# Attention block: the softmax denominators' partial sums shared anew between VectorE and GpSimd, and the unit's order laid out again

## The chip, the core and the metric

One NeuronCore of a Trainium2 chip runs the whole kernel. It has a matrix engine (TensorE), a vector engine (VectorE), an activation engine (ScalarE), a general engine (GpSimd) and SyncE, from whose queue all DMAs are issued here. Each engine works through its own instructions in order and waits on semaphores. The metric is the device time of one execution in microseconds (us).

## The reference

```python
x = L0_attn_q                                   # (4, 1024, 128)
xn = layernorm(x)
xq, xk, xv = rope(xn @ Wq), rope(xn @ Wk), xn @ Wv   # 16 heads of 64; k and v have half the width
xk, xv = repeat(xk, 2, axis=-1), repeat(xv, 2, axis=-1)
scores = softmax(xq @ xk * scale, axis=-1)      # per head, 1024 queries by 1024 keys
attn = (scores @ xv) @ Wo
ffn = (silu(xn @ w_gate.T) * (xn @ w_up.T)) @ w_down.T
return x + attn + ffn
```

Everything is float32. The repetition doubles equal columns, so the kernel works with 32 dimensions per head.

## The kernel before

**Stages.** Up to about 110 us the kernel normalises, transposes x, makes the feed-forward part and the first projections. Then come 32 units (`UNITS`, numbered u): four batches, four groups of four heads, two halves of 512 queries. The loops are unrolled, and each engine has a function `slot` that lists its work for one unit. Unit 31 (`LAST`) has lists of its own.

**One unit.** There are eight tiles of 128 keys (kt = 0 to 7) and four heads (h). TensorE computes the scores of tile kt and head h into one of two PSUM banks (`score`, L553); a score waits until the exponential two before it has read the bank. ScalarE writes exp(score) to `prob` (L871), a ring of four key tiles. TensorE multiplies a finished tile with v (`pv`, four heads side by side, L407). The row maxima of the *next* unit are made beside this: 16 maxima a unit, each from two matmuls (`max_tile`, L392) into one of two places, read by VectorE's row maximum (`reduce_tile`, L950); maximum matmul m waits until maximum m-2 is read. VectorE then splits the maxima into a high and a low part (`split_max`: a cast at L956, a difference at L958), TensorE transposes them (L399), and a DMA puts them beside the queries. The unit also makes projections for a unit three or four later (`project_chunk`, L374; `project_v`, L382), which VectorE rotates (`rotate`, six operations, L941 to L945), ScalarE rounds to a high part (`round_hi`, L757, two halves) and GpSimd subtracts to a low part (`split_lo`, L1125, two halves). SyncE packs both into the score operands.

**The denominators.** A row's denominator is the sum of its exponentials over eight key tiles. Before the change GpSimd adds tiles 0 and 1 (L1173), then 2, then 3; VectorE adds tiles 4 and 5 to `prob_pair` (`pair_sum`, L1043), GpSimd adds this pair and then tile 6 (all L1181). Tile 7 is not added: TensorE sums over the keys with a matrix of ones in two passes, tile 7 (L417) and the partial sum (L420). Behind it come a copy (`read_den`), a transposition (L427), the inversion on VectorE (`invert`, behind row maximum `INVERT_AFTER`), a spread, a transposition back (L434), the product with the output (`normalise`, behind row maximum `NORMALISE_AFTER`) and, one unit later, the output projection (`project_out`, L443), which ScalarE copies (`read_y`) and GpSimd adds (`add_out`, L1189).

**What sets the order.** It is written out by hand in `slot`, engine by engine, with semaphore waits. A ring tile of `prob` may be overwritten when P·V and the partial sums have read it: before, exponentials of tiles 0 and 1 wait for the pair, of tile 2 for the whole sum of the unit before, of tile 3 for its denominators. `prob_pair` is a single buffer. On GpSimd a unit's list is: both low halves, the output add, five large adds.

## Time and profile before

| | |
|---|---|
| median of 3 runs | 1128.86 us (1128.25 to 1129.79) |
| the profiled execution | 1127.29 us |
| its span, first to last instruction | 1125.4 us |
| granted TensorE clock over the span | 0.991 of full speed |
| busy: TensorE, VectorE, GpSimd, ScalarE | 1090.5, 912.1, 853.3, 722.1 us |
| a middle unit | 31.63 us |

A profile shows one execution. Its busy time is a mean over stages, so the table of stretches and the timelines below are read for one unit. Recorded times of instructions overlap a little at their ends: of two neighbours the distance between their starts tells the cost.

### The profile page before, as it was taken

To read this page: it belongs to the slowest core of one execution; us is meant where nothing else is said; L and a number is where in the kernel's file an instruction comes from. 1 tells how busy PE (TensorE), PEld (TensorE's weight loads), DVE (VectorE), ACT (ScalarE), POOL (GpSimd) and SP (SyncE) were. 2 spreads that over 40 slices of the span, in tenths; PEclk is the share of its full clock that TensorE was granted. 3 is DMA by queue.
4 is the path that set the end of the run, shared out by engine and by line. 5 is a ranking of instruction groups with operands and counts; after the bars stand their busy time and mean duration, and the time that the engine had idled before them with its cause. 6 is when DMAs were issued, how large, how long until landed. Compare 5 with 4: busy or idle time off the path is not lost.

```text
span 1125.4 us, 17086 instructions
## 1 busy us (share of the span) xinstructions
PE 1090.5 (97%) x6288; PEld 661.9 (59%) x6288; DVE 912.1 (81%) x1023; ACT 722.1 (64%) x1327; POOL 853.3 (76%) x268
## 2 busy tenths in 40 slices
PE   5899999999999999999999999999999999999987
PEld 4787455666656565656656565656666565654533
DVE  7686878888888888888888888888888888887755
ACT  3333666666666676667666676667666676666664
POOL 3321878888888888888888888888888888888770
PEclk9899999999999999999999999999999999999998
DMA  6662907144260817154260817153260817140000
GB/s 238 159 246 101 269 1 196 38 150 121 48 186 2 232 38 205 29 142 129 50 183 2 232 38 205 29 155 117 51 183 2 232 38 202 32 109 26 4 2 19
DMA packets 56338, 124.98 MB, mean 111 GB/s; under 512 B 8000, under 2 KB 19520, under 8 KB 54080
## 3 DMA queue, kind: packets, MB, share of 16 engines
q1 hardware_dynamic: 56256, 123.90, 37.8%
q8 instruction: 51, 0.84, 0.3%
q14 instruction: 31, 0.25, 0.1%
HBM read 53.08 MB, written 10.49 MB: 56 GB/s over the span
## 4 chain that ended last, share of the span: by engine, by line
PE 93%; DVE 4%; ACT 2%; DMA 1%; issue 1%; ACTq 0%; DVEq 0%
PE bank_s L553 24%; PE scores L392 22%; PE bank_o L407 21%; PE scores L374 8%; PE bank_m L382 3%; PE bank_m L417 3%; PE bank_m L420 2%; PE bank_m L443 2%; PE scores L493 2%; PE bank_s L510 1%; PE bank_m L427 1%; PE bank_m L434 1%; DVE row_max L950 1%; PE bank_o L510 1%; PE bank_m L510 1%
## 5 line engine op out<-in xcount | busy, mean ns | idle before, releaser
L871 ACT ACTIVATE prob<-bank_s 128x512 f32<-128x512 f32 x992 | 566.2, 599 | 274.0 <-PE bank_s L553 263.9
L950 DVE TENSOR_REDUCE row_max<-scores 128x1 f32<-128x1024 f32 x512 | 601.2, 1215 | 97.0 <-PE scores L392 92.9
L1181 POOL TENSOR_TENSOR prob_sum<-prob_sum,prob 128x2048 f32<-128x2048 f32 x93 | 427.1, 4592 | 13.4
L553 PE MATMUL bank_s<-qk_pack 98*128 98x512 f32 x992 | 393.4, 427 | 3.4 <-ACT prob L871 2.0
L392 PE MATMUL scores<-qk_pack 96*128 96x512 f32 x1024 | 323.4, 402 | 2.4 <-DVE rope L945 1.7
L553 PEld LDWEIGHTS bank_s<-qk_pack 98*128 98x128 f32 x992 | 178.2, 188 | 176.2 <-ACT prob L871 117.5
L407 PE MATMUL bank_o<-prob,v 128*32 128x512 f32 x2048 | 254.4, 603 | 0.0
L392 PEld LDWEIGHTS scores<-qk_pack 96*128 96x128 f32 x1024 | 184.6, 189 | 61.1 <-DVE row_max L950 28.8
L1181 POOL TENSOR_TENSOR prob_sum<-prob_sum,prob_pair 128x2048 f32<-128x2048 f32 x31 | 142.5, 4596 | 80.9 <-DVE prob_pair L1043 80.9
L1173 POOL TENSOR_TENSOR prob_sum<-prob 128x2048 f32<-128x2048 f32 x31 | 142.2, 4587 | 0.0
L1125 POOL TENSOR_TENSOR qk_stage<-rope,qk_stage 128x512 fp32r<-128x512 f32 x64 | 81.8, 1280 | 77.9 <-ACT qk_stage L757 77.8
L407 PEld LDWEIGHTS bank_o<-prob,v 128*32 128x32 f32 x2048 | 50.5, 109 | 112.4 <-issue 89.4
L374 PE MATMUL scores<-x_stage,w_stage 128*128 128x512 f32 x336 | 96.7, 396 | 0.0
L374 PEld LDWEIGHTS scores<-x_stage,w_stage 128*128 128x128 f32 x336 | 63.7, 190 | 14.7
L1043 DVE TENSOR_TENSOR prob_pair<-prob 128x2048 f32<-128x2048 f32 x31 | 70.8, 2284 | 0.0
L1189 POOL TENSOR_TENSOR y_acc<-y_part,y_acc 128x512 f32<-128x512 f32 x31 | 39.6, 1278 | 23.2 <-ACT y_part L849 23.2
L1047 DVE RECIPROCAL den_inv<-bank_m 128x16 f32<-128x16 f32 x31 | 8.0, 258 | 60.5 <-PE bank_m L427 60.5
L382 PEld LDWEIGHTS bank_m<-w_stage,x_stage 128*128 128x128 f32 x336 | 46.2, 191 | 4.8
L941 DVE TENSOR_TENSOR scores<-scores,table 128x512 f32<-128x512 f32 x64 | 44.2, 691 | 2.5 <-PE scores L374 2.5
L945 DVE TENSOR_TENSOR rope<-scores,rope 128x512 f32<-128x512 f32 x64 | 44.2, 691 | 2.2
L382 PE MATMUL bank_m<-w_stage,x_stage 128*128 128x128 f32 x336 | 43.8, 267 | 0.0
L943 DVE TENSOR_TENSOR rope<-scores,table 128x512 f32<-128x512 f32 x64 | 43.6, 681 | 0.1
(105 smaller groups left out, 754.3 us busy)
## 6 DMA issues: line engine op xcount, KB each, us to landing
qk_pack<-qk_stage SPq DMA_DIRECT2D x384, 128.0 KB, 4.5
table<-tables SPq DMA_DIRECT2D x16, 2048.0 KB, 9.7
w_stage<-w_scratch SPq DMA_DIRECT2D x14, 640.0 KB, 4.7
v<-v_stage SPq DMA_DIRECT2D x32, 256.0 KB, 7.4
xT_scratch<-xT_hl SPq DMA_DIRECT2D x4, 1024.0 KB, 9.2
x_stage<-xT_scratch SPq DMA_DIRECT2D x4, 1024.0 KB, 6.6
w_scratch<-w_split SPq DMA_DIRECT2D x1, 2560.0 KB, 15.1
x_all<-x SPq DMA_DIRECT2D x4, 512.0 KB, 11.7
```

The costliest lines, as they stand in the source:

```text
L374: last = mm(scores[:, c, :], w_from[:, a, c, :], x_from[:, r, cols], start=n == 0, stop=n == 2)
L382: last = mm(bank_m[:, j * 128:(j + 1) * 128], x_from[:, r, at:at + 128], w_from[:, a, 4, :], start=n == 0, stop=n == 2)
L392: last = mm(scores[:, 2 * (m % places) + c, :], qk_pack[n][0:SPLIT_K, 0, t, h, (m % QT) * 128:(m % QT + 1) * 128], qk_pack[n][0:SPLIT_K, 1 ...
L407: last = mm(bank_o[h * E:(h + 1) * E, :], v_sb[n][:, kt, h * E:(h + 1) * E], prob[:, kt % RING, h, :], start=kt == 0, stop=kt == KT - 1)
L553: mm(bank_s[:, h % 2, :], qk_pack[j][0:SCORE_K, 1, kt // QT, h, (kt % QT) * 128:(kt % QT + 1) * 128], qk_pack[j][0:SCORE_K, 0, t, h, :], s ...
L871: A(prob[:, kt % RING, h, :], bank_s[:, h % 2, :], ACT.Exp).then_inc(prob_ready, 1)
L941: V.tensor_tensor(scores[:, 2 * k, :], scores[:, 2 * k, :], table[:, t, 2 * k, :], ALU.mult).then_inc(rope_read, 1)
L950: V.tensor_reduce(row_max[:, m:m + 1], scores[:, at:at + 2, :].rearrange("p c k -> p (c k)"), axis=AX.X, op=ALU.max).then_inc(max_read, 1)
L1043: V.tensor_tensor(prob_pair[:], prob[:, 4 % RING], prob[:, 5 % RING], ALU.add).then_inc(pair_done, 1)
L1125: TT(qk_stage[:, 2 * k + 1, t, :], rope[:, 2 * k, :], qk_stage[:, 2 * k, t, :].bitcast(F32), ALU.subtract).then_inc(lo_done, 1)
L1173: TT(prob_sum[:, t], prob[:, 0], prob[:, 1], ALU.add).then_inc(sum_done, 1)
L1181: TT(prob_sum[:, t], prob_sum[:, t], part, ALU.add).then_inc(sum_done, 1)
```

## The change

VectorE gets a second pair a unit, tiles 6 and 7 (`last_pair_sum`), into the same buffer `prob_pair`; it stands behind the first row maximum of the next unit and waits until GpSimd has added the first pair. GpSimd no longer adds tile 6 alone; it adds the second pair in the next unit, between the two low halves. The output add moves behind the first large add. The denominators are one pass over the finished sum. The waits of the exponentials follow: tiles 0 and 1 wait for the first pair of the unit before, tiles 2 and 3 for its second pair. `pv` of tile 6 moves with tile 7 into the next unit; TensorE's maxima, P·V groups, transpositions and projections are put in another order; ScalarE's roundings and copies come at other exponentials; the inversion comes behind row maximum 10 and the normalisation behind 15.

```diff
-INVERT_AFTER = 7
-NORMALISE_AFTER = 14
+INVERT_AFTER = 10
+NORMALISE_AFTER = 15
...
 def denominators(u, t):
-                for h in range(HG):
-                    mm(bank_m[h * E:(h + 1) * E, :], ones[:], prob[:, (KT - 1) % RING, h, :], start=True, stop=False)
                 pe.wait_ge(sum_done, 5 * u + 5)
                 for h in range(HG):
-                    last = mm(bank_m[h * E:(h + 1) * E, :], ones[:], prob_sum[:, t, h, :], start=False, stop=True)
+                    last = mm(bank_m[h * E:(h + 1) * E, :], ones[:], prob_sum[:, t, h, :], start=True, stop=True)
...
-                def pv_last():
+                def pv_rest():
                     if not is_first(u):
+                        pv(u - 1, KT - 2, j if t == 1 else 1 - j)
                         pv(u - 1, KT - 1, j if t == 1 else 1 - j)
...
 ScalarE, exponentials:
                         if kt < 2:
-                            act.wait_ge(pair_done, u)
-                        elif kt == 2:
-                            act.wait_ge(sum_done, 5 * u)
-                        elif kt == 3:
-                            act.wait_ge(den_ready, u)
+                            act.wait_ge(pair_done, 2 * u - 1)
+                        elif kt < 4:
+                            act.wait_ge(pair_done, 2 * u)
...
-                        if (kt, h) == (0, 2) and staged:
+                        if (kt, h) == (0, 0) and staged:
                             round_hi(0, u + 3, 1 - t, s + 1 + t)
...
+                        elif (kt, h) == (0, 3) and staged:
+                            round_hi(1, u + 3, 1 - t, s + 1 + t)
...
 VectorE:
+            def last_pair_sum(u):
+
+                dve.wait_ge(prob_ready, NE * KT * (u + 1))
+                dve.wait_ge(sum_done, 5 * u + 4)
+                V.tensor_tensor(prob_pair[:], prob[:, 6 % RING], prob[:, 7 % RING], ALU.add).then_inc(pair_done, 1)
...
                 for m in range(TILES):
                     reduce_tile(u + 1, m)
+                    if m == 0 and not is_first(u):
+                        last_pair_sum(u - 1)
...
 GpSimd:
+            def add_pair(u, t, n):
+
+                pool.wait_ge(pair_done, 2 * u + 1 + n)
+                pool.wait_ge(sum_done, 5 * u + 3 + n)
+                TT(prob_sum[:, t], prob_sum[:, t], prob_pair[:], ALU.add).then_inc(sum_done, 1)
...
-                if not (last_pair and (j, t) != (0, 0)):
-                    split_lo(u + 3, 1 - t)
+                staged = not (last_pair and (j, t) != (0, 0))
+                if staged:
+                    split_lo(u + 3, 1 - t, range(0, 1))
+                if not is_first(u):
+                    add_pair(u - 1, 1 - t, 1)
+                if staged:
+                    split_lo(u + 3, 1 - t, range(1, 2))
+                add_first(u, t)
                 if not is_second(u):
                     add_out(u - 2, t, (u - 2) // UNITS_B)
-                add_probs(u, t)
+                add_next(u, t)
+                add_pair(u, t, 0)
```

TensorE's new order of a unit, where S is a score (tile, head), M a maximum, PV a P·V, D the denominators, V half of the v projection, O the output projection, C a projection chunk, T a transposition, and M0' the first maximum of the unit after next:

```
0: S00 S01 M1 V S02 M2 S03 PV6 PV7 (of the unit before)
1: S10 M3 S11 M4 S12 O S13 M5
2: S20 M6 S21 D M7 S22 S23 M8 PV0
3: S30 M9 S31 T(den) S32 M10 S33 M11
4: S40 PV1 S41 M12 S42 M13 S43 T(inv)
5: S50 M14 S51 S52 M15 S53 PV2 PV3
6: S60 S61 C0 C1 T(max) S62 S63 C2 C3
7: S70 S71 PV4 PV5 S72 S73 M0' V
```

## Rows read from the trace of the kernel before

**Rows 1.** The page's first part: busy time and share of each engine.

```profile
PE 1090.5 (97%) x6288; PEld 661.9 (59%) x6288; DVE 912.1 (81%) x1023; ACT 722.1 (64%) x1327; POOL 853.3 (76%) x268
```

**Rows 2.** Units 1, 10, 28, 29: length, busy time by engine, clock, DMA share, GB/s.

```profile
141.87:173.41 31.54, 31.50 (x180) 17.91 (x179) 25.89 (x28) 21.19 (x39) 24.22 (x7) 1.00 0.01 2
426.47:458.10 31.63, 31.63 (x187) 18.96 (x187) 26.73 (x28) 21.68 (x40) 26.68 (x9) 1.00 0.73 206
995.81:1026.25 30.44, 29.30 (x169) 15.81 (x169) 23.08 (x23) 21.11 (x40) 25.49 (x9) 1.00 0.51 124
1026.25:1056.23 29.98, 29.46 (x161) 15.11 (x162) 22.03 (x22) 20.00 (x38) 24.75 (x7) 1.00 0.01 4
```

**Rows 3.** Timeline of TensorE in unit 10: start, duration, line, tiles, count.

```profile
435.01 1.06 PE L417 MATMUL bank_m<-prob,ones 128*32 128x512 f32 x8
435.89 1.04 PE L420 MATMUL bank_m<-prob_sum,ones 128*32 128x512 f32 x8
...
446.42 0.48 PE L553 MATMUL bank_s<-qk_pack 98*128 98x512 f32 x1
...
447.21 0.40 PE L553 MATMUL bank_s<-qk_pack 98*128 98x512 f32 x1
```

**Rows 4.** Timeline of VectorE where units 9 and 10 meet, and in the tail.

```profile
419.17 1.13 DVE L956 CAST max_hl<-row_max 128x16 fp32r<-128x16 f32 x1
...
420.43 2.28 DVE L1043 TENSOR_TENSOR prob_pair<-prob 128x2048 f32<-128x2048 f32 x1
...
426.48 2.35 DVE L950 TENSOR_REDUCE row_max<-scores 128x1 f32<-128x1024 f32 x2
...
1095.64 2.97 DVE L1081 TENSOR_TENSOR prob_sum<-prob_sum,prob 128x2048 f32<-128x2048 f32 x1 [0.78 <-ACT prob L915]
```

**Rows 5.** Timeline of GpSimd over units 9 and 10.

```profile
403.73 1.28 POOL L1125 TENSOR_TENSOR qk_stage<-rope,qk_stage 128x512 fp32r<-128x512 f32 x1 [2.00 <-ACT qk_stage L757]
...
406.21 4.59 POOL L1173 TENSOR_TENSOR prob_sum<-prob 128x2048 f32<-128x2048 f32 x1
410.94 9.34 POOL L1181 TENSOR_TENSOR prob_sum<-prob_sum,prob 128x2048 f32<-128x2048 f32 x2
422.80 4.60 POOL L1181 TENSOR_TENSOR prob_sum<-prob_sum,prob_pair 128x2048 f32<-128x2048 f32 x1 [2.52 <-DVE prob_pair L1043]
427.54 4.59 POOL L1181 TENSOR_TENSOR prob_sum<-prob_sum,prob 128x2048 f32<-128x2048 f32 x1
432.09 1.28 POOL L1125 TENSOR_TENSOR qk_stage<-rope,qk_stage 128x512 fp32r<-128x512 f32 x1
```

**Rows 6.** By line: shortest, median, longest (ns), first and last start; two timeline rows.

```profile
L956 DVE CAST max_hl<-row_max x32: 174/1134/1161, 101.3 to 1080.4; 128x16 fp32r<-128x16 f32 x32
...
1095.18 1.28 POOL L1189 TENSOR_TENSOR y_acc<-y_part,y_acc 128x512 f32<-128x512 f32 x1 [2.85 <-ACT y_part L849]
...
L1130 POOL TENSOR_TENSOR w_split<-w_raw,w_split x3: 1569/1577/1706, 15.3 to 18.9; 128x640 fp32r<-128x640 f32 x3
...
14.63 0.96 DVE L1013 TENSOR_TENSOR wgu<-y_acc,wgu 128x768 fp32r<-128x768 f32 x1 [0.63 <-ACT wgu L787]
...
L950 DVE TENSOR_REDUCE row_max<-scores x512: 1161/1215/1226, 45.5 to 1079.1; 128x1 f32<-128x1024 f32 x171
```

**Rows 7.** Timeline: two scores on TensorE, their exponentials, a high part's cast on ScalarE.

```profile
411.06 0.70 PE L553 MATMUL bank_s<-qk_pack 98*128 98x512 f32 x2
...
411.57 1.09 ACT L871 ACTIVATE prob<-bank_s 128x512 f32<-128x512 f32 x2 [0.37 <-PE bank_s L553]
...
429.06 0.61 ACT L757 CAST qk_stage<-rope 128x512 fp32r<-128x512 f32 x1
```

**Rows 8.** Timeline of the last unit: denominators, score, exponential.

```profile
1095.16 1.43 PE L417 MATMUL bank_m<-prob,ones 128*32 128x512 f32 x8 [2.02 <-ACT y_part L849]
...
1098.22 1.15 PE L685 MATMUL bank_s<-qk_pack 98*128 98x512 f32 x2
1099.13 1.08 ACT L915 ACTIVATE prob<-bank_s 128x512 f32<-128x512 f32 x2 [3.52 <-PE bank_s L685]
```

More of the change, by code:

```diff
@@ L592, in slot @@
                     if kt == 0:
+                        score(kt, 1)
                         if is_first(u):
@@ L596, in slot @@
                         maximum(1)
-                        score(kt, 1)
                         second_half_v()
@@ L601, in slot @@
                         score(kt, 3)
+                        pv_rest()
+                    elif kt == 1:
                         maximum(3)
-                    elif kt == 1:
-                        pv_last()
+                        score(kt, 1)
                         maximum(4)
-                        score(kt, 1)
-                        maximum(5)
                         score(kt, 2)
@@ L611, in slot @@
                         score(kt, 3)
+                        maximum(5)
+                    elif kt == 2:
                         maximum(6)
-                    elif kt == 2:
-                        maximum(7)
                         score(kt, 1)
@@ L617, in slot @@
                             denominators(u - 1, 1 - t)
+                        maximum(7)
                         score(kt, 2)
@@ L620, in slot @@
                         maximum(8)
+                        pv(u, 0, j)
+                    elif kt == 3:
+                        maximum(9)
+                        score(kt, 1)
                         if not is_first(u):
                             transpose_den(u - 1)
-                        maximum(9)
-                    elif kt == 3:
-                        score(kt, 1)
-                        pv(u, 0, j)
-                        pv(u, 1, j)
+                        score(kt, 2)
+                        maximum(10)
+                        score(kt, 3)
+                        maximum(11)
+                    elif kt == 4:
+                        pv(u, 1, j)
+                        score(kt, 1)
+                        maximum(12)
+                        score(kt, 2)
+                        maximum(13)
+                        score(kt, 3)
+                        if not is_first(u):
+                            transpose_inv(u - 1)
+                    elif kt == 5:
+                        maximum(14)
+                        score(kt, 1)
+                        score(kt, 2)
+                        maximum(15)
+                        score(kt, 3)
+                        pv(u, 2, j)
+                        pv(u, 3, j)
+                    elif kt == 6:
+                        score(kt, 1)
+                        project_chunk(0)
+                        project_chunk(1)
+                        at_least(pe, o_done, u)
+                        transpose_max(v)
@@ L653, in slot @@
                         project_chunk(2)
-                        score(kt, 3)
                         project_chunk(3)
-                        at_least(pe, o_done, u)
-                        transpose_max(v)
                     else:
                         score(kt, 1)
-                        for n in (4, 5, 6):
-                            pv(u, n, j)
+                        pv(u, 4, j)
+                        pv(u, 5, j)
                         score(kt, 2)
@@ L1083, in last_slot @@
             def last_slot():
+                last_pair_sum(LAST - 1)
                 dve.wait_ge(den_ready, LAST - 1)
@@ L1120, in _, with split_lo @@
             TT = nc.gpsimd.tensor_tensor
-            def split_lo(w, t):
-                for k in range(2):
+            def split_lo(w, t, halves=range(2)):
+                for k in halves:
                     pool.wait_ge(hi_done, 2 * w + k + 1)
@@ L1173, in add_probs, with add_next @@
                 TT(prob_sum[:, t], prob[:, 0], prob[:, 1], ALU.add).then_inc(sum_done, 1)
-                for n, kt in enumerate((2, 3, 4, 6)):
-                    if kt == 4:
-                        pool.wait_ge(pair_done, u + 1)
-                    else:
-                        pool.wait_ge(prob_ready, NE * (KT * u + kt + 1))
-                    pool.wait_ge(sum_done, 5 * u + n + 1)
-                    part = prob_pair[:] if kt == 4 else prob[:, kt % RING]
-                    TT(prob_sum[:, t], prob_sum[:, t], part, ALU.add).then_inc(sum_done, 1)
+            def add_next(u, t):
+                for n, kt in enumerate((2, 3)):
+                    pool.wait_ge(prob_ready, NE * (KT * u + kt + 1))
+                    pool.wait_ge(sum_done, 5 * u + n + 1)
+                    TT(prob_sum[:, t], prob_sum[:, t], prob[:, kt % RING], ALU.add).then_inc(sum_done, 1)
+            def add_pair(u, t, n):
+                pool.wait_ge(pair_done, 2 * u + 1 + n)
+                pool.wait_ge(sum_done, 5 * u + 3 + n)
+                TT(prob_sum[:, t], prob_sum[:, t], prob_pair[:], ALU.add).then_inc(sum_done, 1)
             def add_out(u, t, b):
@@ L1205, in _ @@
             pairs_of_steps(body)
+            add_pair(LAST - 1, 0, 1)
             add_out(LAST - 2, 1, B - 1)
```

54 lines of the change are left out of this document (13 added, 41 removed).

## The prediction

> **What bounds the kernel now.** I read the page's busy shares first: TensorE is busy 97% of the span, VectorE 81%, GpSimd 76%, ScalarE 64% [rows 1]. The table of stretches then shows where that holds. In a middle unit (one head group, half the queries) TensorE is busy for all of its 31.63 us, at the full granted clock, while VectorE has 26.73 and GpSimd 26.68 us of work [rows 2]. So today the unit is as long as TensorE's list, and each of the other two has 4.9 us to spare. The reader should not stop there: spare time helps only where no order of waits uses it up. So I went on to the timelines of VectorE and GpSimd and looked for a ring of work that runs through both.
>
> **What TensorE saves.** The first four-head pass of the denominators (eight instructions) begins 0.88 us before the second [rows 3]; the change leaves one pass. Nothing else leaves TensorE: the second P·V of the last pair of tiles only moves into the next unit, and there are five P·V groups in a unit before and after, so the switches between P·V and score matmuls stay the same in number. TensorE's list becomes 31.63 - 0.88 = 30.75 us. The new order adds waits of its own. A score's bank is free again only when its exponential is done: that starts 0.51 us after the score and takes 0.60 (of a pair 1.09 us long, the second ends 0.5 after the first) [rows 7]. Scores 0 and 2 of stage 5 now have one score and one maximum between them, and a score and a maximum take 0.79 us together [rows 3], so with the second score about 1.0; the bank needs about 1.2. I take 0.3 us a unit for this and the score behind it (estimate; ends 0, if the loads run ahead, and 0.9). **TensorE alone: about 31.05 us.** If that were the bound, 26 middle units (2 to 27) would give back 26 x 0.58 = 15 us.
>
> **What VectorE gets.** One more add of 128x2048, which lasts 2.28 us as the present pair does [rows 4]: 26.73 + 2.28 = 29.01 us, still under 31.05. It stands behind the first row maximum of the next unit, with fifteen maxima queued behind it, on which TensorE's maximum matmuls 3 and 4 wait. The inversion, for which VectorE today stands idle, moves from behind maximum 7 to behind maximum 10, so this idle time pays for most of the pair.
>
> **What GpSimd gets.** The same five large adds and three small ones; a pair takes the place of tile 6. But the pair's add moves into the next unit, between the two halves of the low-part subtraction (I call them lo0 and lo1). GpSimd waits there for VectorE, with lo1, the first add and all of the unit's sum queued behind it; the one denominator pass on TensorE waits for it in turn. No DMA is moved; SyncE packs a head when lo1 is done, which comes at about the same place of the unit as before, and lo0 earlier.
>
> **Two engines at one door.** The cast of the row maxima (16 columns) takes 0.174 us at its shortest and 1.134 in the median [rows 6]. In the middle unit it begins at 419.17, lasts 1.13 and ends at 420.30 [rows 4]; GpSimd's adds of tiles 2 and 3 end at 410.94 + 9.34 = 420.28 [rows 5]. In the tail a VectorE add with both inputs in SBUF lasts 2.97 us where the pair lasts 2.28 [rows 4]; it begins at 1095.64, inside a GpSimd add that runs from 1095.18 to 1096.46 [rows 6]. So VectorE's cast and its SBUF+SBUF adds stand still until about 0.15 us before the GpSimd operation ends. The other way round there is one row: GpSimd's first weight subtraction starts at 15.3, while a VectorE add with two SBUF inputs runs until 15.59, and takes 1.706 us where the others take 1.57 [rows 6]: it ends at VectorE's end plus its own length less 0.14. The row maxima, which read PSUM, show no such stretch: 1161 to 1226 ns from the shortest to the longest [rows 6].
>
> The Trainium skill says the same of the mechanism (SBUF — State Buffer, § Who interferes with whom): a VectorE instruction with two SBUF inputs contends with a GpSimd instruction that reads SBUF, and the one that comes second fully blocks. It speaks against this change, which puts a second such add into the one stretch where GpSimd has something ready to run. Both directions agree with rows 6; without the rule the sum would be TensorE's 31.05.
>
> **Who meets whom now.** In the new order the second pair starts on VectorE about 1 us into the unit. lo0 needs the first exponential (0.51 + 0.6) and the high part's cast behind it (0.61) [rows 7], so it is ready at about 1.7 and finds VectorE in the middle of its 2.28 us. lo0 therefore ends at the pair's end + 1.28 - 0.14 = +1.14, and the pair's add on GpSimd starts 1.10 us behind VectorE's end, not 0.09 (today's step from 420.43 + 2.28 = 422.71 to 422.80 [rows 4, 5]).
>
> **The ring, step by step**, from the start of the pair's add on GpSimd: this add 4.55 (427.54 to 432.09 [rows 5]); lo1 1.24 (two small operations take 403.73 to 406.21, 2.48); the first add 4.55; the output add 1.24; tiles 2 and 3, 9.34. Sum 20.92. Behind its end: cast, difference, first pair and rope run without a gap on VectorE until the next row maximum, 420.28 to 426.48 = 6.20 [rows 4, 5]. Then that maximum 1.15 (two take 2.35), the second pair 2.28, and 1.10 to the next start. **20.92 + 6.20 + 1.15 + 2.28 + 1.10 = 31.65 us.** A second ring, through GpSimd's own add of the first pair (7.12 from 420.28 to 427.40) in place of rope and maximum, gives 20.92 + 7.12 + 0.09 + 2.28 + 1.10 = 31.51. So the bound passes from TensorE (31.63) to a ring through GpSimd and VectorE of the same length, and TensorE gets waits of about 0.5 us a unit, at the transposition of the maxima above all, which waits for the late cast. **A middle unit stays at 31.63, within 0.1.** What the denominators give back is lost again before the cast.
>
> **The ends.** Unit 1 has no output add, so its ring is 31.65 - 1.24 = 30.4 where it took 31.54 [rows 2]: -1.1. Unit 28 has no projection to fill TensorE but still lo0 and lo1: from the second pair's end, the transposition comes at 4.5 + 20.92 + 0.4 = 25.8 behind the first maximum, and the last scores, P·V and exponentials behind it take about 5.4 (estimate from the same spacings): 31.1 against 30.44 [rows 2]: +0.7. Units 29 and 30 have no lo0 and lo1, so the ring is shorter there by more than 2 us and TensorE bounds them: 0.88 saved, about 0.5 of it lost behind the second pair, against 29.98 today [rows 2]: -0.4 each, -0.8. In the last unit TensorE waits 2.02 us in front of the denominators, and the pass from 1095.16 to 1098.22 takes 3.06 us; the exponentials of tile 3 follow at 1099.13 [rows 8]. Half a pass goes (some 1.4 us), one more P·V pushes the scores ahead of it back by about as much as the wait leaves over: -1.0 (ends -2.5 and +0.5). Unit 0 is unchanged. **Together -2.2 us.**
>
> The profiled execution took 1127.29 us, a span of 1125.40 and 1.89 around it; the median of the runs is 1128.86, 1.57 above. 1127.29 - 2.2 = 1125.1 in such an execution, **1126.6 as a median; I say 1126.5.**
>
> **Rivals.** (a) *GpSimd is not held while VectorE adds the pair.* Only 0.28 us of overlap in one row speaks for the hold in that direction. Then the step of 1.10 is 0.09, the ring 30.64, and TensorE bounds at 31.05: 26 x -0.58 = -15, with the ends some -16 to -17: 1112. (b) *The hand-over is dearer.* If lo0 runs its whole length behind the pair, a unit has 0.14 more: +3.6 - 2.2, 1130.3. It decides from 0.17 us a unit: (2.2 + 2.3) / 26.
> The Trainium skill's figure, in the same page (§ A bandwidth-pool intuition that's wrong), is a start about 115 ns behind VectorE's end; that would be 0.26 a unit and 1133; no row here shows it.
> (c) *TensorE loses its slack* and ends slower: the second pair holds maxima 1 and 2 back by 2.2 us, maximum matmuls 3 and 4 wait for them, and VectorE, with 29 us of work, cannot catch up, so later maxima, the exponentials' banks and the denominators come late together. Price: all waits of TensorE beyond 0.9 a unit; it is slower from 0.17 above that. At 1.2, the unit is 31.95: 26 x 0.32 - 2.2 = +6.1, 1135. For it: two lists of 29 and 31 us in lock step with two score buffers. Against: by the order written out, each maximum finds its buffer read. (d) *It does not do what it says*: the denominators' one pass waits for a sum that comes later than today's. It is due at about 9 us of the unit and the ring has the sum at 4.5 + 4.6 = 9.1: under 0.2, inside TensorE's slack; no case of its own.
>
> **Chances.** Forecast ring 0.58 (0.28 faster, 0.27 inside 0.2%, 0.03 slower); (a) 0.15, faster; (b) 0.13 (0.05 same, 0.08 slower); (c) 0.10 (0.02 same, 0.08 slower); the rest 0.04 (0.02 faster, 0.02 slower). Faster 0.45, same 0.34, slower 0.21; 0.2% (2.3 us) is about what a measurement of this kernel can tell from no change. The likeliest case alone holds 1124 to 1130; the range reaches to (a) and to the near part of (b) and (c): 1112 to 1132.
>
> **What would show it.** Middle units of 31.5 to 31.8; GpSimd's lo0 drawn out or begun behind VectorE's second pair; the cast still ending with GpSimd's add of tile 3; TensorE waiting for the difference of the maxima. If middle units are at 31.1 with lo0 inside the pair, (a) is right; if the maxima wait for TensorE and TensorE for the maxima, (c).

## The result, and the profile after

The changed kernel takes 1135.59 us (median of 20 executions, 1128.61 to 1144.03) where the kernel before takes 1129.23 (20, 1127.81 to 1135.23): the ratio is 1.0055, with a 95% interval of 1.0037 to 1.0073. It is slower by half a per cent; the forecast was 1126.5, with a range up to 1132. The execution that was profiled took 1132.50 us with a span of 1130.7, 5.3 more than the span before.

The page's first part, as in [rows 1]:

```profile
PE 1084.1 (96%) x6040; PEld 649.0 (57%) x6040; DVE 1007.9 (89%) x1054; ACT 718.8 (64%) x1327; POOL 887.7 (79%) x268
```

TensorE has lost 248 instructions (a pass of 8 in each of 31 units), VectorE has 31 more. The stretches that answer to [rows 2], cut at the same instruction (the first score behind the next unit's first maximum matmul and its value projection, where there is one; I call that maximum M0', a unit's own M1 to M15): units 1, 10, 28, 29 and 30. Columns: length, busy time of TensorE, its loads, VectorE, ScalarE and GpSimd, then the granted clock, DMA share and GB/s.

```profile
142.80:176.91 34.11, 34.00 (x171) 19.25 (x171) 27.89 (x29) 21.38 (x39) 26.29 (x7) 0.90 0.00 1
429.76:461.42 31.66, 31.25 (x179) 18.42 (x179) 29.91 (x29) 21.51 (x40) 27.96 (x9) 1.00 0.74 206
999.11:1031.71 32.60, 30.19 (x162) 15.54 (x161) 26.00 (x23) 21.22 (x40) 28.52 (x9) 0.95 0.47 116
1031.71:1061.63 29.92, 28.99 (x153) 14.74 (x154) 24.46 (x23) 20.36 (x38) 23.25 (x6) 1.00 0.01 4
1061.63:1093.17 31.54, 30.19 (x152) 14.55 (x152) 24.46 (x22) 20.37 (x38) 24.89 (x7) 0.95 0.01 2
```

Unit 30 of the kernel before, by the same cut, had a stretch at the lower clock too:

```profile
1056.23:1087.84 31.61, 30.61 (x159) 15.00 (x160) 21.99 (x21) 20.02 (x38) 25.65 (x8) 0.95 0.00 1
```

With the starts of the units this gives the whole balance. The last column is an experiment's, told below.

| us against the kernel before | forecast | changed | changed, M0' waiting for head 0 only |
|---|---|---|---|
| up to unit 1 (141.87 before) | 0 | +0.93 | -1.99 |
| unit 1 (31.54) | -1.1 | +2.57 | -0.54 |
| units 2 to 27 together (822.40) | 0 | -0.20 | -0.23 |
| unit 28 (30.44) | +0.7 | +2.16 | +1.89 |
| unit 29 (29.98) | -0.4 | -0.06 | 0.00 |
| unit 30 (31.61) | -0.4 | -0.07 | -1.69 |
| last unit (37.56) | -1.0 | -0.03 | +0.06 |
| span (1125.4) | -2.2 | +5.3 | -2.5 |

Each kernel was profiled once more later. Units 1 and 28 of those executions by the same cut, first of the changed kernel, then of the kernel before:

```profile
142.16:176.32 34.16, 34.05 (x172) 18.78 (x171) 27.81 (x29) 21.41 (x39) 26.52 (x7) 0.90 0.00 1
998.40:1029.36 30.96, 28.54 (x161) 15.38 (x161) 26.03 (x23) 21.22 (x40) 27.25 (x9) 1.00 0.50 122
```

```profile
142.12:173.68 31.56, 31.52 (x180) 17.88 (x179) 25.87 (x28) 21.17 (x39) 24.53 (x7) 1.00 0.01 2
997.37:1029.48 32.11, 30.99 (x170) 16.13 (x169) 23.06 (x23) 21.10 (x40) 27.17 (x9) 0.95 0.48 118
```

Unit 1 is longer in the changed kernel in both pairs (+2.57 and +2.60). Unit 28 is not: it was +2.16 and is -1.15, and it is long in whichever execution has the lower clock there. Up to unit 1 the pairs differ by +0.93 and +0.04.

**The middle is as forecast.** VectorE, GpSimd and TensorE of the changed kernel, where units 10 and 11 meet and a little later:

```profile
462.35 2.28 DVE L1044 TENSOR_TENSOR prob_pair<-prob 128x2048 f32<-128x2048 f32 x1
463.17 2.60 POOL L1129 TENSOR_TENSOR qk_stage<-rope,qk_stage 128x512 fp32r<-128x512 f32 x1 [1.04 <-ACT qk_stage L757]
...
465.73 4.59 POOL L1190 TENSOR_TENSOR prob_sum<-prob_sum,prob_pair 128x2048 f32<-128x2048 f32 x1
...
477.30 9.33 POOL L1184 TENSOR_TENSOR prob_sum<-prob_sum,prob 128x2048 f32<-128x2048 f32 x2
...
484.40 2.27 DVE L951 CAST max_hl<-row_max 128x16 fp32r<-128x16 f32 x1
...
487.02 0.27 PE L399 MATMUL bank_m<-ident,max_hl 128*32 128x128 f32 x1 [0.31 <-DVE max_hl L953]
```

lo0, 1.28 us long in [rows 5], is drawn out to 2.60 and ends 1.14 behind the second pair (462.35 + 2.28 = 464.63); the pair's add on GpSimd starts 1.10 behind it. The cast stands still till GpSimd's add of tile 3 ends (486.63). TensorE waits 0.31 for the difference of the maxima. All of this is what the ring said.

**The ends are not.** TensorE at M0' of unit 0, at unit 28's transposition of the maxima (T(max)) with the P·V group behind it, and at the last unit's denominators:

```profile
141.64 0.71 PE L392 MATMUL scores<-qk_pack 96*128 96x512 f32 x2 [2.08 <-issue]
...
1024.68 0.27 PE L399 MATMUL bank_m<-ident,max_hl 128*32 128x128 f32 x1 [1.64 <-DVE max_hl L953]
...
1026.93 3.57 PE L407 MATMUL bank_o<-prob,v 128*32 128x512 f32 x16
...
1101.37 1.39 PE L418 MATMUL bank_m<-prob_sum,ones 128*32 128x512 f32 x8 [2.03 <-ACT y_part L849]
```

In the kernel before, M0' of unit 0 also waited, but less:

```profile
140.71 0.70 PE L392 MATMUL scores<-qk_pack 96*128 96x512 f32 x2 [1.68 <-DVE rope L945]
```

The stretches around the first wait, of the changed kernel, and the last of them in the kernel before:

```profile
110.00:115.00 5.00, 4.12 (x12) 2.68 (x11) 3.70 (x4) 4.59 (x8) 4.77 (x3) 0.71 0.37 89
115.00:120.00 5.00, 5.00 (x14) 3.39 (x12) 4.42 (x4) 3.03 (x6) 3.77 (x3) 0.61 1.00 291
...
140.00:145.00 5.00, 3.36 (x15) 2.91 (x16) 2.62 (x2) 1.83 (x4) 0.21 (x1) 0.78 0.01 5
145.00:150.00 5.00, 5.00 (x25) 2.44 (x24) 3.17 (x3) 2.45 (x5) 5.00 (x2) 0.53 0.00 0
```

```profile
145.00:150.00 5.00, 4.96 (x23) 2.36 (x21) 4.75 (x5) 4.27 (x10) 1.61 (x3) 1.00 0.01 3
```

The granted clock is 0.53 in 145 to 150 us: most of it at the lower level, 1.2 instead of 2.4 GHz. In the kernel before it was 1.00 there. The two P·V groups of unit 28, 1.92 us long elsewhere, last 3.57.

### The profile page after: what moved, and what is told of

Same layout as the page of the kernel before. It is cut to its first block, busy times and chain, and to the rows that moved or that the text cites. A ratio compares the mean times of both kernels' runs of the same rounds, so it can differ in the third digit from the quotient of the medians.

```text
span 1130.7 us, 16653 instructions
## 1 busy us (share of the span) xinstructions
PE 1084.1 (96%) x6040; PEld 649.0 (57%) x6040; DVE 1007.9 (89%) x1054; ACT 718.8 (64%) x1327; POOL 887.7 (79%) x268
## 4 chain that ended last, share of the span: by engine, by line
PE 75%; DVE 19%; issue 4%; ACT 1%; DMA 1%; ACTq 0%; DVEq 0%
PE bank_s L551 19%; PE scores L392 18%; PE bank_o L407 17%; DVE row_max L945 9%; DVE max_hl L951 5%; PE scores L374 4%; PE bank_m L382 3%; PE bank_m L418 3%; PE bank_m L441 2%; PE scores L491 2%; DVE o_norm L1054 2%; PE bank_s L508 1%; PE bank_m L425 1%; PE bank_o L508 1%; PE bank_m L399 1%
## 5 line engine op out<-in xcount | busy, mean ns | idle before, releaser
L869 ACT ACTIVATE prob<-bank_s 128x512 f32<-128x512 f32 x992 | 573.3, 599 | 319.7 <-PE bank_s L551 301.4
L551 PE MATMUL bank_s<-qk_pack 98*128 98x512 f32 x992 | 400.2, 433 | 5.8 <-ACT prob L869 2.2
L1190 POOL TENSOR_TENSOR prob_sum<-prob_sum,prob_pair 128x2048 f32<-128x2048 f32 x62 | 284.4, 4587 | 89.5 <-DVE prob_pair L1038 79.5
L392 PE MATMUL scores<-qk_pack 96*128 96x512 f32 x1024 | 330.9, 404 | 2.5 <-issue 2.1
L1184 POOL TENSOR_TENSOR prob_sum<-prob_sum,prob 128x2048 f32<-128x2048 f32 x62 | 284.5, 4589 | 4.7
L407 PE MATMUL bank_o<-prob,v 128*32 128x512 f32 x2048 | 257.8, 610 | 0.0
L1129 POOL TENSOR_TENSOR qk_stage<-rope,qk_stage 128x512 fp32r<-128x512 f32 x64 | 117.8, 1843 | 53.0 <-ACT qk_stage L757 52.9
L374 PE MATMUL scores<-x_stage,w_stage 128*128 128x512 f32 x336 | 86.4, 392 | 0.0
L1044 DVE TENSOR_TENSOR prob_pair<-prob 128x2048 f32<-128x2048 f32 x31 | 70.7, 2282 | 5.8 <-ACT prob L869 5.8
L1038 DVE TENSOR_TENSOR prob_pair<-prob 128x2048 f32<-128x2048 f32 x31 | 70.8, 2284 | 0.0
L951 DVE CAST max_hl<-row_max 128x16 fp32r<-128x16 f32 x32 | 62.6, 1956 | 0.1
```

The lines of the kernel that those rows point to most:

```text
L374: last = mm(scores[:, c, :], w_from[:, a, c, :], x_from[:, r, cols], start=n == 0, stop=n == 2)
L392: last = mm(scores[:, 2 * (m % places) + c, :], qk_pack[n][0:SPLIT_K, 0, t, h, (m % QT) * 128:(m % QT + 1) * 128], qk_pack[n][0:SPLIT_K, 1 ...
L407: last = mm(bank_o[h * E:(h + 1) * E, :], v_sb[n][:, kt, h * E:(h + 1) * E], prob[:, kt % RING, h, :], start=kt == 0, stop=kt == KT - 1)
L551: mm(bank_s[:, h % 2, :], qk_pack[j][0:SCORE_K, 1, kt // QT, h, (kt % QT) * 128:(kt % QT + 1) * 128], qk_pack[j][0:SCORE_K, 0, t, h, :], s ...
L869: A(prob[:, kt % RING, h, :], bank_s[:, h % 2, :], ACT.Exp).then_inc(prob_ready, 1)
L951: V.tensor_copy(max_hl[:, 0, :].bitcast(F32R), row_max[:]).then_inc(max_hi, 1)
```

## Experiments

Three questions: whether the ring sets the middle unit; which of TensorE's waits lose the time at the ends; whether the two add up to a version that beats both kernels. A median is given beside that of the kernel before on the same chip.

### Does the ring set the middle unit?

**lo0 cut to 8 columns** (the low part of the other query columns is left out).

```diff
+ n = 8 if len(halves) == 1 and k == 0 else HALF
- TT(qk_stage[:, 2*k+1, t, :], rope[:, 2*k, :], ...
+ TT(qk_stage[:, 2*k+1, t, 0:n], rope[:, 2*k, 0:n], ...
```

> The first of the two differences that GpSimd makes in a middle slot (query low part) is cut to 8 of 512 columns; the low part of the other columns is left out, so old values stand there. What is left is the whole order, with that instruction as good as gone. Theory R (the ring of the prediction): GpSimd's second-pair add then starts at the end of VectorE's add and not 1.10 us behind it, the ring is 30.55 us, and TensorE with 31.05 us of work binds the middle unit: 31.05 to 31.15 instead of 31.62, 27 units x 0.5 = 13 to 15 us less than the changed kernel, T(max) of a middle unit without its 0.3 us wait. If another chain sets 31.62 (the order of the scores, packing), the unit stays 31.5 to 31.7 and the time within 2 us of the changed kernel's.

Measured: 1117.22 (before 1130.18), ratio 0.9898 (0.9847 to 0.9949). The second pairs start 31.00 us apart in the middle, not 31.62. The timeline of GpSimd and VectorE at the cast:

```profile
467.11 9.31 POOL L1185 TENSOR_TENSOR prob_sum<-prob_sum,prob 128x2048 f32<-128x2048 f32 x2
...
475.29 1.17 DVE L951 CAST max_hl<-row_max 128x16 fp32r<-128x16 f32 x1
```

The cast still ends with GpSimd's add of tile 3 (476.42), but no T(max) waits: TensorE's own list binds, at 31.00 where the forecast put it at 31.05. The time is 19 us under the changed kernel's, more than the 13 to 15 expected; a part of that may be M0' of unit 0, which waited only 0.69 us in this profile, with the clock at 1.00 from 140 to 150 us.

**Both low-part differences behind the second-pair add.**

```diff
-                if staged:
-                    split_lo(u + 3, 1 - t, range(0, 1))
                 if not is_first(u):
                     add_pair(u - 1, 1 - t, 1)
                 if staged:
-                    split_lo(u + 3, 1 - t, range(1, 2))
+                    split_lo(u + 3, 1 - t)
```

> The changed kernel with both low-part differences behind GpSimd's second-pair add; nothing left out. A second test of the ring's arithmetic, in the other direction: the hold of 1.10 us goes, 0.09 and lo0's own length of 1.28 come: 31.62 - 1.10 + 0.09 + 1.28 = 31.89 us for a middle unit. If instead what matters is that lo0 stands before the pair at all (its wait for the high part), the unit gets shorter, 31.0 to 31.3.

Measured: units of 31.83 from start to start; one execution, 1140.85 us. VectorE's and GpSimd's timeline at the second pair:

```profile
467.07 2.28 DVE L1044 TENSOR_TENSOR prob_pair<-prob 128x2048 f32<-128x2048 f32 x1
469.43 4.57 POOL L1190 TENSOR_TENSOR prob_sum<-prob_sum,prob_pair 128x2048 f32<-128x2048 f32 x1 [2.57 <-DVE prob_pair L1044]
473.97 2.52 POOL L1129 TENSOR_TENSOR qk_stage<-rope,qk_stage 128x512 fp32r<-128x512 f32 x2
```

The add starts 0.08 behind the pair, lo0 costs its own length, and the unit is 0.06 from the sum. The ring's arithmetic holds in both directions.

**lo0 made by VectorE**, behind its second pair (nothing left out).

```diff
 last_pair_sum(u - 1)
+first_lo(u, u + 3, 1 - t)      # on VectorE, behind row maximum 0
...
-split_lo(u + 3, 1 - t, range(0, 1))
 add_pair(u - 1, 1 - t, 1)
+second_lo(u, u + 3, 1 - t)     # GpSimd, lo1 only
```

> Nothing left out: the same first difference is made by VectorE, right behind its add of tiles 6 and 7, and GpSimd goes from the second-pair add straight to the second difference. Theory R: VectorE's difference (512 columns, about a quarter of the 2.28 us of the pair, 0.6 us) holds GpSimd's add by 0.6 us instead of 1.10, ring 31.15 us, VectorE's own work 29.6: unit 31.1 to 31.2, 11 to 14 us less than the changed kernel (about 1122 to 1125). Rival: GpSimd's 4.6 us add gets in first and VectorE's difference stands still till it ends; then each unit is up to 4 us longer, 1230 us.

Measured: 1129.36 (before 1130.18), ratio 0.9989 (0.9961 to 1.0017); middle units of 31.46. The timeline of VectorE, GpSimd and TensorE at the second pair:

```profile
496.23 1.23 DVE L946 TENSOR_REDUCE row_max<-scores 128x1 f32<-128x1024 f32 x1 [0.40 <-PE scores L393]
497.37 2.28 DVE L1045 TENSOR_TENSOR prob_pair<-prob 128x2048 f32<-128x2048 f32 x1
499.57 0.69 DVE L1049 TENSOR_TENSOR qk_stage<-rope,qk_stage 128x512 fp32r<-128x512 f32 x1
499.73 4.95 POOL L1202 TENSOR_TENSOR prob_sum<-prob_sum,prob_pair 128x2048 f32<-128x2048 f32 x1 [3.07 <-DVE prob_pair L1045]
...
502.57 0.73 PE L393 MATMUL scores<-qk_pack 96*128 96x512 f32 x2 [0.16 <-DVE row_max L946]
```

VectorE's 0.69 us hold GpSimd's add by 0.36 (4.95 against 4.59), so the ring by itself is short enough. What misses the 31.15 is that VectorE now waits in it for TensorE: row maximum 0 stands 0.40 us for its matmuls. On TensorE maximum matmul 3 waits 0.16 us for a row maximum that the 0.69 us push back; what else makes its list 31.46 and not 31.00 is not shown. One unit took 35.89 us from the start of one cast to the next: its M0', at 272.24, had waited 1.45, and the clock of 275 to 280 us was 0.50. That gave the next question.

### Which waits lose the time at the ends?

**The changed kernel again.**

> The changed kernel as it is, for a second profile and for the times of the same chip. Theory A (clock): in the first profile every middle unit, from one second-pair add to the next, took 31.62 us, and the 5.3 us that the span was longer by lay where TensorE's granted clock stood below 1.00 (110 to 120 us, 140 to 150, 1025 to 1030, the last unit). So a second profile keeps 31.62 in the middle units, and the stretches below 1.00 lie behind waits of TensorE again, at the ends or at T(max) in a middle unit; a slower run has a lower mean clock. Theory B (order): the loss is work and waits that the new order adds, the same in each run; then the second profile shows units 0, 1 and 28 longer by the same amounts with the clock at 1.00.

Measured: 1136.19 (1128.82 to 1142.22; before 1130.18), ratio 1.0052 (1.0027 to 1.0077). Its profile is of its fastest execution, span 1127.0: the middle at 31.62, the clock 0.72 in 110 to 115 us, 0.79 and 0.52 in 140 to 150 behind a wait of 2.00 at M0'. Behind T(max) of unit 28, which waited 1.68, the clock stayed at 1.00. The slowest execution has the lower mean clock, 0.980 against 0.989.

**Unread matmuls in the waits.**

```diff
+def fill(bank, n, w=0):
+    for _ in range(n):
+        mm(bank, qk_pack[w][0:SPLIT_K, 0, 0, 0, 0:128], qk_pack[w][0:SPLIT_K, 1, 0, 0, :], ...)
...
+if is_first(u): fill(bank_o[:], 4)     # before the first scores, and again behind M1
+if is_first(u): fill(bank_m[:], 8)     # before M0'
+if last_pair: fill(scores[:, c, :], 3, j)   # c = 0, 1, before T(max)
```

> The changed kernel with matmuls whose results nobody reads put into TensorE's waits: 4 before the first scores and 4 behind M1 of unit 0, 8 before M0' of unit 0 (it waited 2.08 us there), and 6 before T(max) in units 28, 29 and 30, where the query chunks are missing (T(max) of unit 28 waited 1.64 us). They add about 0.21 to 0.26 us each, nearly all inside waits whose ends do not move. Theory A (clock): granted clock 1.00 in 110 to 150 us and 1020 to 1030 us; unit 1's cast some 2.6 us earlier, the PV group behind T(max) of unit 28 at 1.9 instead of 3.6 us: together 4 to 6 us less than the changed kernel on this chip, and a narrower spread from run to run. Theory B (order): the waits end when they ended and nothing is gained: 0 to 2 us more than the changed kernel.

Measured: 1127.58 (1125.76 to 1130.76; before 1130.18), ratio 0.9975 (0.9957 to 0.9993). More work, 8.6 us less time than the changed kernel beside it where 4 to 6 were expected, and a spread of 5 us instead of 13. TensorE's timeline at M0':

```profile
141.96 0.70 PE L392 MATMUL scores<-qk_pack 96*128 96x512 f32 x2 [0.67 <-issue]
```

and the stretches around it:

```profile
140.00:145.00 5.00, 4.33 (x25) 3.52 (x24) 2.30 (x2) 1.66 (x4) 0.13 (x1) 1.00 0.03 11
145.00:150.00 5.00, 5.00 (x29) 2.30 (x27) 4.74 (x5) 3.98 (x9) 5.00 (x2) 1.00 0.02 3
```

M0' starts 0.32 later than in the changed kernel, and the next cast comes 2.84 earlier (165.90, not 168.74): with the same work behind M0', that is the clock. **The start alone, and the ends alone:**

> Only the matmuls at the start of the earlier filled kernel: 4 before the first scores, 4 behind M1 and 8 before M0' of unit 0. If the loss and the spread sit at the start, where every profile of the changed kernel showed the clock below 1.00 in 110 to 120 us and 140 to 150 us: 1128 to 1130, spread like the fully filled kernel's (5 us). If they sit at the ends (T(max) of unit 28) as much: half of the 8.6 us that the full filling gave, 1131 to 1133, and a spread of 8 us or more.

> Only the 6 matmuls before T(max) in units 28, 29 and 30. The counterpart of the run before it: if the loss sits at the start this leaves 1134 to 1136 and the wide spread (13 us); if it sits at the ends, 1130 to 1132 and a narrow one. The two gains together should come to about the 8.6 us of the full filling.

Measured (before 1129.10): start 1130.88, ratio 1.0005 (0.9983 to 1.0027); ends 1136.57, ratio 1.0064 (1.0039 to 1.0088). The start gives some 5 us (the ratio was 1.0052 without), the ends by themselves nothing, so the two do not add up to the 8.6; and with the start alone the executions still spread over 10 us (1125.14 to 1135.12), not over the 5 expected. Units 28 to 30 show why the ends are worth little: filled, they take 31.00, 30.95 and 30.63 us at a clock of 1.00, 92.58 together, which lies between the two profiles of the changed kernel (94.06 with two falls of the clock, 91.09 with none). What the matmuls save where the clock would have fallen they cost where it would not.

**TensorE's old order in unit 0** (its stages 0 to 5 as in the kernel before; the rest as changed).

> TensorE's order of before in stages 0 to 5 of unit 0 alone (M0 and M1 ahead of the second score, the P.V groups where they were), everything else as changed. Theory A1: the falls at 110 to 120 us come from the new order's gaps at the first scores; with the old order the clock is 1.00 there as in the profile of before, and unit 1's cast comes 1 to 2.5 us earlier. Theory A2: the gap of 0.9 us behind the first scores is the same in both orders (0.89 and 0.88) and whether the clock falls behind it differs from run to run: then falls at 110 to 120 us are seen here too and the time stays within 1.5 us of the changed kernel's.

Measured: 1136.88 (before 1129.10), ratio 1.0056 (1.0023 to 1.0089). Its profile has the clock at 1.00 in 110 to 120 us, but the run of split values below, with the new order, has that too, and **the kernel before in a second profile** has the fall:

> The kernel before once more, for a second profile. Its span was 1125.4 us with the clock at 1.00 from 110 to 1080 us. If the falls behind the waits at 110, 140 and 270 us are the changed kernel's own, none is seen; if they come to both kernels by chance, one of them may be.

Measured: 1130.52 us, span 1128.7. Its timeline of TensorE at M0' of unit 0:

```profile
140.96 0.70 PE L392 MATMUL scores<-qk_pack 96*128 96x512 f32 x2 [1.31 <-DVE rope L945]
```

and its stretches at the first scores and behind M0':

```profile
110.00:115.00 5.00, 4.10 (x14) 2.81 (x13) 3.88 (x4) 4.07 (x6) 4.77 (x3) 0.77 0.29 68
...
140.00:145.00 5.00, 4.04 (x24) 3.59 (x25) 3.07 (x4) 2.53 (x6) 4.86 (x2) 1.00 0.01 2
```

So the fall at 110 to 120 us comes to some executions of both kernels and is not the difference. The one at 140 to 150 is seen in every profile in which M0' of unit 0 waited 2 us or more (2.00 to 3.48, seven profiles of the changed kernel and its variants), in neither of the two of before (1.68 and 1.31), and not in the run with the short lo0 (0.69).

**What M0' waits for.** The values' copies on a semaphore of their own:

```diff
- v_sb[n][...], v_stage[...]).then_inc(packed, 16)
+ v_sb[n][...], v_stage[...]).then_inc(vals_packed, 16)
```

> Nothing left out: the copies of the values count on a semaphore of their own, so that M0' of the next unit waits for the packed heads alone and no longer for the two copies of v (the last one, issued behind all heads, lands some 7.8 us after its issue, a head's rows 4.7 us). M0' of unit 0 waited 2.08 and 2.00 us, and in three other runs a middle M0' waited 0.5 to 1.9 us with the engine's own sequence at an end. If the v copy is what comes last there: M0' waits under 0.3 us everywhere, the clock stays 1.00 in 140 to 150 us, and the time falls by 2 to 5 us with a narrower spread. If the heads come last, the wait stays 2 us and the time is the changed kernel's.

Measured: 1134.69 (before 1129.10), ratio 1.0044 (1.0024 to 1.0064). M0' of unit 0 still waits 2.43: it is not the values alone. In unit 4 it waits again, by TensorE's timeline:

```profile
273.77 0.70 PE L393 MATMUL scores<-qk_pack 96*128 96x512 f32 x2 [1.73 <-DVE rope L943]
```

and the clock falls in the stretch behind it:

```profile
275.00:280.00 5.00, 5.00 (x18) 4.14 (x17) 4.07 (x3) 2.73 (x5) 2.52 (x2) 0.50 0.00 0
```

That unit lasts 38.22 us instead of 31.62 from the start of one cast to the next (the filled ends' profile has the same, 38.44); from end to end it is 36.58, since GpSimd no longer holds the late cast. The row names the rope, which ended at 272.84, 0.93 before M0' started; so it was another wait. The times in the trace at which copies land tell which: the last head lands at 141.49 us in unit 0 and at 273.68 in unit 4, each 0.09 before M0' starts, and the values only at 142.08 and 274.29. So the heads hold M0' in this run. In the changed kernel one counter stands for heads and values, and M0' starts 0.09 behind the last landing of either (141.54; in the kernel before 140.62); which of the two that was its trace cannot tell. **M0' therefore waits for the one head it reads** (nothing left out):

```diff
-pack_head(n, t, h, packed)
+pack_head(n, t, h, packed0 if h == 0 else packed)
...
-pe.wait_ge(packed, 16 * PACKS * (s + 1))       # before M0'
+pe.wait_ge(packed0, 16 * 6 * (s + 1))
...
+if t == 1: pe.wait_ge(packed, 16 * PACKS * (s + 1))   # before M4 of the next unit
```

> The changed kernel, nothing left out: M0' of the next unit reads head 0 alone, and now waits for head 0's packed rows only; M4 of the next odd unit, the first to read another head, waits for the rest. If M0's wait for the heads (2.0 to 3.5 us in unit 0 in every profile of the changed order, and at times 1 to 2 us in unit 4) with the clock's fall behind it is what makes the change slower, the wait is gone, the clock stays 1.00 from 140 to 1020 us, unit 1's cast comes 3 to 5 us earlier and the median falls from 1135 to 1129 to 1131, with an upper end at 1135 and not 1144. If the falls come by themselves at the start and not from this wait, the median stays at 1134 to 1136.

> The kernel before with M0' waiting for head 0 alone. Its M0' waited 1.68 and 1.31 us in unit 0 and 1.01 in a middle unit, without a fall. If the kernel before loses to these waits only the wait itself: 0.5 to 1.5 us less in the median (1128), the upper end from 1135 down to 1131. If its slower executions come from elsewhere (the first scores, T(max) of unit 28): no narrower.

Measured (before 1128.47): the changed kernel with it 1128.09 (1124.49 to 1129.16), ratio 0.9982 (0.9968 to 0.9996); the kernel before with it 1128.01, ratio 0.9986 (0.9971 to 1.0000). Of the first, the stretches behind M0' of unit 0, then units 1, 2 to 27, 28, 29 and 30:

```profile
140.00:145.00 5.00, 5.00 (x32) 2.89 (x33) 4.91 (x4) 3.57 (x7) 3.32 (x2) 1.00 0.00 2
...
139.88:170.88 31.00, 30.87 (x169) 17.51 (x170) 28.27 (x29) 21.14 (x39) 26.17 (x7) 1.00 0.01 2
170.88:993.05 822.17, 812.21 (x4605) 478.65 (x4604) 777.16 (x729) 559.16 (x1040) 725.06 (x208) 1.00 0.40 112
993.05:1025.38 32.33, 30.06 (x162) 15.65 (x161) 25.98 (x23) 21.27 (x40) 28.50 (x9) 0.95 0.48 117
1025.38:1055.36 29.98, 28.95 (x154) 14.75 (x154) 24.48 (x23) 20.36 (x38) 23.24 (x6) 1.00 0.01 4
1055.36:1085.28 29.92, 28.54 (x152) 14.37 (x152) 24.42 (x22) 20.36 (x38) 24.09 (x7) 1.00 0.01 2
```

and TensorE's timeline at M0':

```profile
138.55 0.63 PE L393 MATMUL scores<-qk_pack 96*128 96x512 f32 x2
```

M0' no longer waits (head 0 had landed at 136.35), no middle unit is over 31.7, and the median is 7 to 8 us under the changed kernel's, which was not run beside it: the ratio to the kernel before goes from 1.0055 and 1.0052 to 0.9982. Unit 1's cast comes 6.03 us earlier (162.71): 3.09 of it before M0', 2.94 behind it, at the clock. The kernel before gains only 0.5; in its profile another wait, of 1.16 for the packed maxima in front of unit 1's scores, brought the clock down to 0.70 and 0.62 at the same place, and unit 1's cast came at 168.28. So it was M0's wait that made the changed kernel slower, and with it gone the change itself gives nothing that can be measured: 1128.09 against 1128.01. **The kernel before with the start filled:**

> The kernel before with the same matmuls at its start: 4 before the first scores, 4 behind M1, 7 before M0' of unit 0 (it waited 1.68 us there, the clock stayed at 1.00 in its profile). If the start's falls are the changed kernel's own: same median as before within 1 us. If the kernel before has them too, only in fewer executions: the lowest times stay at 1127, the upper end comes down from 1134 to 1136 to about 1131, the median by 0.5 to 2 us.

Measured: 1128.70 (1127.40 to 1129.90; before 1129.07, 1126.93 to 1138.81), ratio 0.9988 (0.9967 to 1.0008): the lowest stay, the upper end comes down, and the median does not move clear of noise. The kernel before can lose in the same way, as its profile with head 0 shows; that it does so more seldom is read from its upper end alone.

### A version that beats both

lo0 on VectorE with the waits filled, and with M0' waiting for head 0, without and with the filled start and ends:

> Nothing left out: VectorE makes the first low-part difference (middle unit 31.46 us in its own run), and the unread matmuls of the filled kernel stand in TensorE's waits (4 and 4 at the first scores, 8 before M0' of unit 0, 6 before T(max) in units 28 to 30), with 5 more before M0' of unit 4, where three profiles showed a wait of 1.5 to 2.0 us and a unit 4 to 7 us longer behind it. If both findings add: 1129.4 less about 6 to 8 us, 1121 to 1124, spread within 6 us, the clock at 1.00 up to the last unit. If the falls behind waits are not what the filling cured: 1128 to 1131 as without it.

> The same, with VectorE making the first low-part difference (middle unit 31.46). Without M0's waits its median should be 1129.4 less 5 to 6 us: 1123 to 1125, and no middle unit over 32.5 us. If the middle falls have another cause: 1128 to 1130 as before.

> Both of these, and unread matmuls at the first scores of unit 0 (4 and 4) and before T(max) in units 28 to 30 (6 each). The falls at 110 to 120 us and behind T(max) of unit 28 cost some 2 us each in the profiles that had them: 1120 to 1123. If filling gave what it gave through M0' alone: 1123 to 1125.

Measured: 1127.90, ratio 0.9982 (0.9966 to 0.9998), outside what was expected: M0' of unit 20 waited 2.92 with nothing to fill it, 37.37 us for that unit; 1123.52, ratio 0.9954 (0.9938 to 0.9970); 1122.59, ratio 0.9940 (0.9918 to 0.9962), the lowest of those that leave nothing out, though its interval overlaps that of the run without filling. The last two are below the kernel before; the changed kernel, at 1.0055, was not run beside them. The stretch of the last one from the second pair of unit 2 to that of unit 28 (26 units of 31.50), at full clock throughout:

```profile
172.98:991.94 818.96, 812.04 (x4603) 479.56 (x4602) 761.64 (x755) 561.98 (x1041) 668.55 (x182) 1.00 0.40 112
```

## Why the prediction was wrong

**Right: TensorE's list, the door, the ring.** 31.05 us for TensorE alone was 31.00; the hold of 1.10 us is in the rows; the ring of 31.65 was 31.62, and both runs that altered it moved it by its own terms (31.83 against 31.89 expected; 31.00 at TensorE's bound). T(max) took up the slack, 0.3 us a unit. Rival (a) is out. So is (b): lo0 ends 1.14 behind the pair, its own length less 0.14, and the unit did not grow. The Trainium skill's 115 ns (SBUF — State Buffer, § A bandwidth-pool intuition that's wrong) would by an estimate (1.28 + 0.115) have put lo0's end 1.40 behind; the trace shows 1.14, and the measurement decides. Rival (c) had the right time, 1135, by luck: no middle unit is longer.

**Wrong: the ends, and there the words "Unit 0 is unchanged".** The forecast priced the ends at the full clock and asked only for GpSimd, VectorE and TensorE's own list. It put M0' of unit 0 at nothing, which already waited 1.68 us in the kernel before, for the last of the copies of heads and values that SyncE issues. "No DMA is moved" was true, and SyncE issued its last head copy at the same time (135.84 against 135.74). But TensorE's list of unit 0 is not unchanged: P·V of tile 6 moves from it into unit 1, as the prediction says of every unit (two groups take 1.92 us, one 1.06), and a TensorE that comes sooner only waits longer for the same landings. In the profiles with the clock at 1.00 up to M0' of unit 0, TensorE comes to it 28.8 us behind its first score where tile 6 is moved (filled ends, lo0 last, values on their own, and TensorE's old order in stages 0 to 5) and 29.3 and 29.5 us behind it where it is not (before with head 0, before). So 0.5 to 0.7 us go into the wait, which was 2.08 and 2.00 us in the two profiles of the changed kernel and 1.68 and 1.31 in those of before.

In the first profiles M0' also started 0.93 later, but that is not the new order's: in the second ones it starts at 140.99 against 140.96. The table of DMA issues from 110 to 143 us has 6.1 us in the median from issue to landing of the heads in the changed kernel's first profile, 5.6 in its second and 5.3 with head 0, and 5.2, 5.5 and 5.9 in the same three of the kernel before. Why the copies land no sooner, when SyncE begins the last twelve 1.52 us earlier (123.75, not 125.27), was not settled.

Behind the longer wait TensorE ran at the lower clock: from M0' to the next cast 27.10 us, where it takes 24.16 (M0' for head 0 alone) or 23.94 (filled). So unit 0 at nothing and unit 1 at -1.1 were together +3.5 in the first profiles and +2.6 in the second. With the wait out they are -2.5: -1.99 of it comes up to unit 1, for the most part the wait, which the kernel before had too (1.68), and unit 1 gives -0.54, since TensorE's 31.05 binds it and not the ring's 30.4, a bound that the prediction's own sum for unit 1 left out.

**Unit 28** was +0.7 by the ring (its two parts, 25.8 and 5.4, make 31.2 and not 31.1) and +2.16 in the first profile. In the second, at a clock of 1.00, it takes 30.96 us, +0.5: T(max) waits 1.68 us, as the late cast and the missing chunks make it, and the ring is about right. The other 1.6 are the fall of the clock, in which the two P·V groups run 1.65 longer (3.57, not 1.92); the kernel before has such a fall in its second profile (32.11 us). **Units 29 and 30** gave nothing (-0.4 each); unit 30 differs only by whether a fall of the clock lies in it. **The last unit** gave 0.0 (-1.0): its denominators start 8.20 us into the unit instead of 7.32 and still wait 2.03 for ScalarE's copy, as in [rows 8]; that copy is behind the work that was pushed back.

**The chances.** No rival had a wait of TensorE that costs more than its own length. The profiles of the changed kernel explain a part of the loss: 2.6 to 3.5 us up to the end of unit 1. In the median it lies 3.1 us above its first profiled execution, the kernel before 1.9 above its own; the slower executions have the lower clock. Profiles of neighbours show how such an execution loses 4 to 7 us more, at M0' of unit 4 or 20; no profile of the changed kernel itself caught one, so that this is its tail as well is inferred, from the spread that went when the wait went. Why unit 4 waits in some profiles and not in others stays open.

## What to carry to other kernels

Where an engine is busy all the time, look for its rare waits before pricing a change to its order: a wait of 2 us behind which its clock fell cost the wait and 3 us more here, which is more than all that the forecast hoped to gain (2.2 us). Ask also where saved time goes: in front of a wait for a copy it only makes the wait longer. Ask of each wait what exactly is awaited; here a counter over four heads and the values stood for the one head that was read. And take a spread that widens, with a mean clock that falls, as a sign that the loss is not in the list of work.

## What the runs showed of the hardware

At M0', and in one profile at unit 1's first scores, TensorE's granted clock fell in or behind single waits of 1.2 to 3.5 us in an otherwise full engine, and not always: at M0' in a middle unit it fell behind 1.45, 1.73, 1.86, 2.02 and 2.92 us and stayed at 1.00 behind 1.58, 1.04 and 1.01. Waits of 0.3 us (changed kernel) and 0.6 us (lo0 last) in every middle unit never brought it down. At the first scores of unit 0, with two waits of 0.9 us, it fell in some profiles and not in others. In the last units, where TensorE has less to do, the length of the wait tells even less: at T(max) of unit 28 the clock stayed at 1.00 behind 1.68 us in one profile and fell behind 0.75 in another, and in unit 30 of both kernels it fell with no wait over 0.3 us before it. The Trainium skill describes a kernel whose waits for DMAs bring TensorE to the lower clock again and again (TensorE: Matmul & The Clock Gate, § HAM oscillation — how this bites in real kernels); the trace agrees that a wait for DMAs can do it (2.08 us at M0' of unit 0, a clock of 0.53 behind it), but here it came once or twice in an execution. Unread matmuls in the waits kept the clock up, 8.6 us for some 34 of them.

A VectorE cast that meets a GpSimd add ends with it: the cast of 16 columns lasts 0.17 us at its shortest and 2.27 in the middle unit of the changed kernel. The other way round, GpSimd's difference of 1.28 us that meets VectorE's add of two SBUF tiles ends 1.14 us behind it.
